# The down weights of a channel mix, loaded by pairs of ring slots: one transfer of 1 MB in place of two of 512 KB

## The reference, cut to what matters

```python
xc = _ln(_ln(x2, ln2_g, ln2_b), cm_g, cm_b)
xcs = _shift(xc)
kc = jnp.square(jax.nn.relu(xcs @ Wck))      # 2048 x 512 by 512 x 2048
vc = kc @ Wcv                                # 2048 x 2048 by 2048 x 512
rc = jax.nn.sigmoid(xc @ Wcr)
return x2 + rc * vc
```

## Time and profile before

| | |
|---|---|
| time, median of 3 runs | 1046.41 us (1044.85 to 1047.88) |
| the profiled execution: its own time | 1043.99 us |
| its span in the profile | 1042.2 us |
| PE busy | 1026.3 us, 98% of the span |
| TensorE clock granted | 1.00 of full speed in all slices |
| ring loads (`vring<-wcv_d`) | 64 of 512 KB, 3.3 us from issue to landing in the median |

### The profile page before, as it was taken

One profiled execution on the slowest core, in us unless ns is written; L12 is line 12 of the kernel. 1 busy time (PEld: TensorE's weight loads), 2 busy tenths in 40 slices (PEclk: granted clock), 3 DMA queues, 4 the chain that ended last, 5 costly groups with the idle time before them and its releaser, 6 DMA issues.

```text
span 1042.2 us, 18079 instructions
## 1 busy us (share of the span) xinstructions
PE 1026.3 (98%) x5378; PEld 849.2 (81%) x5378; DVE 656.4 (63%) x1207; ACT 553.8 (53%) x957; POOL 433.4 (42%) x332
## 2 busy tenths in 40 slices
PE   6999999999999999999999999999999999999998
PEld 2556888888888888888887888889999999999986
DVE  7977957915490559051007398967777777777746
ACT  5963646333433343334335343357777777777742
POOL 1022303220222022202223523468888888888533
PEclk9999999999999999999999999999999999999999
DMA  8905296516431643334356692067988999888778
GB/s 291 386 13 200 89 338 220 182 61 243 162 102 61 241 161 101 100 122 162 101 193 236 239 289 85 1 196 152 279 193 247 239 213 318 203 166 173 115 272 343
DMA packets 102389, 195.05 MB, mean 187 GB/s; under 512 B 15544, under 2 KB 39096, under 8 KB 101824
## 3 DMA queue, kind: packets, MB, share of 16 engines
q1 hardware_dynamic: 82944, 158.70, 43.8%
q0 software_dynamic: 18816, 34.64, 17.1%
q10 hardware_dynamic: 576, 1.05, 0.3%
HBM read 141.98 MB, written 63.18 MB: 197 GB/s over the span
## 4 chain that ended last, share of the span: by engine, by line
PE 93%; DMA 2%; DVE 2%; POOL 1%; issue 1%; ACT 0%; POOLq 0%; SPq 0%; ACTq 0%; DVEq 0%
PE bank L686 42%; PE bank L1029 23%; PE bank L1648 14%; PE bank L591 5%; PE bank L1638 4%; DMA hTb<-hT_d 1%; PE bank L651 1%; PE bank L1040 1%; DMA g1b<-in_L_attn_ln_b 1%; PE bank L1100 1%; PE bank L1050 1%; POOL mix_lo L398 0%; PE bank L645 0%; PE bank L628 0%; DVE mx L387 0%
## 5 line engine op out<-in xcount | busy, mean ns | idle before, releaser
L1006 POOL TENSOR_TENSOR ksp_lo<-ra,ksp_hi 128x512 fp32r<-128x512 f32 x94 | 140.7, 1497 | 428.3 <-ACT ksp_hi L949 428.1
L1648 PEld LDWEIGHTS bank<-xT,wus 128*128 128x128 f32 x1344 | 162.8, 191 | 7.1
L1648 PE MATMUL bank<-xT,wus 128*128 128x128 f32 x1344 | 163.5, 275 | 0.0
L1029 PE MATMUL bank<-vring,ksp_hi 128*128 128x512 f32 x512 | 158.5, 391 | 0.0
L686 PE MATMUL bank<-xcT,wck_hi 128*128 128x512 f32 x512 | 158.4, 390 | 0.0
L941 ACT ACTIVATE ra<-bank 128x512 f32<-128x512 f32 x96 | 57.4, 598 | 169.6 <-PE bank L686 167.3
L1800 DVE TENSOR_TENSOR wd_lo<-w,wd_hi 128x1024 fp32r<-128x1024 f32 x84 | 103.0, 1226 | 50.0 <-ACT wd_hi L1728 49.9
L686 PE MATMUL bank<-wd_hi,aT 128*128 128x512 f32 x336 | 125.9, 415 | 0.0
L949 ACT ACTIVATE ksp_hi<-ra 128x512 fp32r<-128x512 f32 x96 | 60.7, 632 | 119.1 <-PE bank L1029 118.6
L686 PEld LDWEIGHTS bank<-xcT,wck_hi 128*128 128x128 f32 x512 | 95.7, 188 | 19.8
L1029 PEld LDWEIGHTS bank<-vring,ksp_hi 128*128 128x128 f32 x512 | 95.4, 188 | 19.5
(11 more groups left out here) (294 smaller groups left out, 1986.5 us busy)
## 6 DMA issues: line engine op xcount, KB each, us to landing
vring<-wcv_d SPq DMA_DIRECT2D x64, 512.0 KB, 3.3
w<-in_L_ffn_Wu SPq DMA_DIRECT2D x32, 512.0 KB, 7.7
w<-in_L_ffn_Wd SPq DMA_DIRECT2D x32, 512.0 KB, 7.7
hT_d<-hT SPq DMA_DIRECT2D x16, 512.0 KB, 3.8
hTb<-hT_d SPq DMA_DIRECT2D x3, 2048.0 KB, 9.1
raw_wcv<-in_L_attn_Wcv SPq DMA_DIRECT2D x4, 1024.0 KB, 6.9
raw_wck<-in_L_attn_Wck SPq DMA_DIRECT2D x4, 1024.0 KB, 9.7
add_d<-zrow SPq DMA_DIRECT2D x1, 4096.0 KB, 20.2
```

Source lines behind the costliest of these rows:

```text
L1006: nc.gpsimd.tensor_tensor(ksp[1][:, i % 2], ra[:, i % 2], ksp[0][:, i % 2], ALU.subtract).then_inc(sem("klo_in"), 1)
L1029: m = nc.tensor.matmul(bank[to + j][:], ksp[l][:, i % 2, j * P:(j + 1) * P], rhs(r), start=i == 0 and k == 0, stop=i == last and k == 2)
L1648: m = nc.tensor.matmul(bank[4 + u][:, n * P:(n + 1) * P], wus[u][:, c * EI + n * P:c * EI + (n + 1) * P], xT4[:, u, c * P:(c + 1) * P], st ...
```

## The change

A ring load now fills two neighbouring slots, chunks i and i+1 for even i, in one transfer of 1 MB, once down(i-3) has ended, which is the last reader of the second slot. ring(i) does nothing for odd i. There are 32 transfers in place of 64 and two semaphores in place of four, one for each pair of slots; down(i) waits for that of its pair.

```diff
             def down(i, rows=range(BT)):
                 if i == 0:
                     pe.wait_ge(sem("u_in"), b * BT + 4)
-                pe.wait_ge(sem(f"vr_in{i % 4}"), 64 * b + 16 * (i // 4) + 16)
+                pe.wait_ge(sem(f"vr_in{i % 4 // 2}"), 64 * b + 16 * (i // 4) + 16)
...
         def sp_block2(sp, b, first=False, last=False):
             def ring(i):
+                if i % 2:
+                    return
                 n = b * NCI + i
                 if not (first and i < 4):
-                    wait_apart(sp, sem("vc_done"), n - 1)
+                    wait_apart(sp, sem("vc_done"), n)
                 if first and i % 4 == 0:
                     sp.wait_ge(sem("wst"), 32 * max(2, i // 4 + 1))
-                sp.dma_start(vring[:, i % 4].bitcast(F), wcv_d[i]).then_inc(sem(f"vr_in{i % 4}"), 16)
+                sp.dma_start(vring[:, i % 4:i % 4 + 2].bitcast(F),
+                             wcv_d[i:i + 2].rearrange("a p m -> p a m")).then_inc(sem(f"vr_in{i % 4 // 2}"), 16)
```

## The result

The changed kernel takes 1046.61 us in the median of 20 executions (1044.46 to 1050.52), the kernel before 1044.42 us in as many. The profiled execution has a span of 1045.2 us, 3.0 us above that of before.

What follows compares the result with a forecast made beforehand. PE, busy 98% of the span, was taken as the bound. To the 1046.41 us median came 1.3 (last pair), 0.1 (first pair) and 0 (all else): 1047.8 us, range 1044.5 to 1050.5.

Steps and rivals of the forecast that it cites:

- The last pair's term: Last block, chunks 14 and 15: 512 KB more ahead of hTb lengthen PE's wait by 1.3 us (0 to 2.0); chance 0.60.
- the queue's order: Queue behind the last ring load: transfers keep their order, so everything behind, quiet 2 us included, moves back 1.3 us.
- the absorbing quiet stretch: Rival: the quiet 2 us behind ring(15) is fixed in time and takes the extra bytes; 1046.4 us, chance 0.21.
- The first pair: First block: PE's first down now needs ring(0) and ring(1), landing at 157.6 against 157.91; cost 0.1 us (0 to 0.9).
- The refills: Steady part: pairs land in about 5 us against a lead of at least 10.9 us; cost 0 for all 32.
- The price formula for late refills: Rival in the steady part: a refill costs its landing time beyond its lead; 1051 or 1090 us, chance 0.07.
- The hT stores: Blocks 1 to 3: chunks 4 and 5 go ahead of them, delaying DVE at most 3.2 us within 21.9 us cover; cost 0.
- the term goes into the time in full: Start of stage 3: all of the 1.3 us added to PE's wait for hTb lengthens the kernel's time.
- nothing is given back later: After 551.09: PE's only waits, 1.5 us for POOL, move with PE, so none of the 1.3 us is recovered.
- larger transfers bring `hTb` forward: Rival in the full queue between 534 and 549: gains at most the 1.2 us wait for hTb; 1045.2 us, chance 0.05.
- The rival of the late first pair: First block: first pair up to 0.9 us late, besides the last pair's term; 1048.7 us, chance 0.07.

Runs made afterwards that it cites:

- the second profile: The changed kernel, unaltered, profiled and timed once more against the kernel before: 1046.36 us, ratio 1.0020 (1.0010 to 1.0030).
- five kernels: Single loads, ebias behind hTb (0.9996); single and paired, hTb early (0.9997, 1.0004); single and paired, hTb, ebias and raw loads early (1.0001, 1.0002).

## Why the prediction was right, and where it was not

**The last pair's term** held in place and size: 1.3 us predicted, 1.2 us in the wait for `hTb` and in the distance from the last ring transfer to stage 3 (0.9 us more wait in the second profile). Its mechanism is shown from both sides, by the last pair alone (2.4 us) and by all but the last (1.1 us). The choice of the queue's order over the absorbing quiet stretch was right: the stretch was forecast to begin at 537.8; it begins at 538.5, or 537.9 without the 0.6 us by which this execution lags. That `ebias` makes it is shown by moving it.

**The first pair** cost nothing, where 0.1 us was taken: it landed at 157.4, 1.1 us before PE's first down.

**The refills** cost nothing that the runs can tell: 4.9 us to landing, forecast 4.5 to 5, against a lead of 10.9 us and more; a lead cut to 8.2 us, and to 5.4 us for three of them, still cost nothing. The price formula for late refills, landing time less lead, gave 56 us for 59.9 measured.

**The hT stores** delayed DVE by 3.7 us less the common 0.6, so 3.1, forecast at most 3.2; PE's transposes moved by no more than the common 0.6 us.

**What goes into the time.** The step "so the term goes into the time in full" was too small a statement. The doubled wait costs its 1.2 us and, in 21 of 29 executions, another 1.6 us of half clock behind it: 1.2 + 0.7 x 1.6 = 2.3 us, for a measured 2.0 (1.0 to 2.9). The sum had no term for the clock at all, and no reason for leaving it out. The 1.4 us predicted lie within the measured interval even so; the count of executions at the lower clock shows the missing term, and not the time alone. With the wait filled by useless work the clock term is gone, and 0.5 us (-0.4 to 1.5) are left, where 1.2 us were expected. The same step said that nothing is given back later. Seen from the changed kernel this held, but seen the other way it didn't: taking the wait for `hTb` away gave no gain clear of noise in five kernels (ratios of 0.9996 to 1.0004), since DVE's `hb` is then late by 1.1 us or more. The rival "larger transfers bring `hTb` forward", priced at 1.2 us, would have met the same.

**The number** was 1047.8 us for 1046.61. The three runs shown of before had a median 2.0 us above that of the 20 taken later, and the step from before to after was forecast 0.8 us too small in the medians (1.4 for 2.2). The two errors have opposite signs, and that they leave only 1.2 us is luck. The rival of the late first pair is 1046.41 + 1.3 + 0.9 = 1048.6 us; its 1048.7 counts the first pair's 0.1 us twice.

## What to carry to other kernels

A transfer that is itself well hidden still has a place in its queue: before making one larger or later, look for the last one of its kind, and for what the critical path loads right behind it. A small load can hold a queue for as long as 0.7 MB would (here 16 KB, 128 bytes to each of 128 partitions, and 1.7 us, at 404 GB/s); put it behind what is urgent. And where the matmul engine is the bound, price a wait by its length and by the clock behind it: 1.2 us more of waiting cost 2 us here, and with most of the wait filled by useless matmuls the kernel was some 1.5 us faster than with PE idle.

## What was not expected of the hardware

The granted clock: with an idle stretch of 1.2 us (the kernel before) the mean clock of an execution was at 0.998 or below in 3 of 35 and 1 of 25, with 2.1 to 2.4 us in 21 of 29, which fits the profile of one of these, 0.50 for about 3.5 us. It doesn't fall in all of them (the first profile, 2.44 us of wait, clock 1.00). The kernel whose refills wait for two downs more lost about 21 us to it, by the estimate above, beside 60 us of waits. Why it falls in some executions and not in others the runs don't settle.

A load of 16 KB to 128 partitions, 128 bytes each, kept the transfers behind it in its queue waiting for 1.6 to 2 us, in which 13 to 20 GB/s moved. Whether its small pieces are the reason no run shows.

A DVE operation of 0.54 us that met a POOL operation of 2.56 us took 2.60 us, and one of 0.16 us that met one of 2.40 us took 2.32 us. They ended within 0.3 us of POOL's.
